# Four graph layers on one core: the tiled matmuls of a step in one run, O and h at its head, the transposed exponentials in its middle

## The reference

```
h  = relu(layernorm(x))                       # 128 x 384
q, k, v = h @ Wq + bq, h @ Wk + bk, h @ Wv + bv     # 6 heads of 64
p  = softmax(q @ k.T / 8, masked by adj)      # 6 x 128 x 128
x1 = x + (p @ v) @ Wf + bf
g  = relu(layernorm(x1))
hh = g @ W                                    # 12 heads of 32
a  = leaky_relu(tanh(hh)@w_src + (tanh(hh)@w_dst).T), no edge: -999
f  = elu(softmax(a) @ hh + b)                 # 12 x 128 x 128
gate = sigmoid(g @ H_w.T + H_b)
x2 = x1 + gate * f + (1 - gate) * g
```

## Time and profile before

| | |
|---|---|
| median of three runs | 2048.41 us |
| the profiled execution | 2048.47 us, of which the span is 2046.4 us |
| PE busy | 1979.5 us (97%) |
| ACT busy | 1953.5 us (95%) |
| DVE busy | 1813.4 us (89%) |
| POOL busy | 1629.2 us (80%) |
| mean granted TensorE clock | 0.988 of 2.4 GHz |
| ACT L525, first and last start | 84.0 and 2018.1 us |

### The profile page before, as it was taken

How to read it: one execution, slowest core, us unless ns; L and a number is a source line. 1 busy time by engine, 2 the same in 40 slices (tenths; PEclk the granted TensorE clock), 3 DMA queues, 4 the chain that set the end, 5 groups by cost and what they waited for, 6 DMA issues and landing times.

```text
span 2046.4 us, 58352 instructions
## 1 busy us (share of the span) xinstructions
PE 1979.5 (97%) x19596; PEld 1845.0 (90%) x19596; DVE 1813.4 (89%) x4117; ACT 1953.5 (95%) x6800; POOL 1629.2 (80%) x2859
## 2 busy tenths in 40 slices
PE   4999999999999999999999999999999999999983
PEld 4899999999999999999999999999999999999972
DVE  4689999999999999999999999999999999999884
ACT  3799999999999999999999999999999999999995
POOL 3478888888888888888888888878888878888864
PEclk9999999999999999999999999999999999999995
DMA  5012223323323222223432222222222222221122
GB/s 170 12 46 67 70 60 79 86 68 91 86 65 83 53 51 57 56 50 82 122 99 58 53 52 60 50 53 61 50 52 61 50 54 60 50 52 49 39 47 50
DMA packets 309330, 130.62 MB, mean 64 GB/s; under 512 B 229547, under 2 KB 308782, under 8 KB 309038
## 3 DMA queue, kind: packets, MB, share of 16 engines
q1 hardware_dynamic: 309038, 126.90, 24.8%
HBM read 69.42 MB, written 57.41 MB: 62 GB/s over the span
## 4 chain that ended last, share of the span: by engine, by line
ACT 49%; DVE 37%; PE 5%; issue 4%; POOL 2%; DMA 1%; DVEq 1%; SPq 1%; POOLq 0%
ACT LG L506 27%; ACT LA L500 14%; DVE LG L636 11%; DVE neg_max L640 10%; DVE LA L613 9%; DVE stats L617 3%; ACT cT_hi L558 2%; ACT QKT L514 2%; ACT v L566 2%; PE psum L731 2%; DVE rdenG L632 1%; DVE rden L611 1%; ACT sdT L572 1%; PE psum L741 1%; DMA xin<-x 1%
## 5 line engine op out<-in xcount | busy, mean ns | idle before, releaser
L506 ACT ACTIVATE LG<-LG,neg_max 128x128 f32<-128x128 f32 x1536 | 595.4, 392 | 15.9 <-DVE neg_max L640 8.8
L500 ACT ACTIVATE LA<-LA,neg_max 128x128 f32<-128x128 f32 x768 | 297.9, 400 | 0.0
L506 ACT ACTIVATION_READ_ACCUMULATOR LG<-LG,neg_max 128x1 f32 x1536 | 291.9, 190 | 0.0
L430 POOL TENSOR_TENSOR prod<-th,vec 128x384 f32<-128x384 f32 x256 | 254.3, 1017 | 6.9 <-ACT th L543 6.9
L636 DVE COPY_PREDICATED_SCALAR LG<-no_edge,no_edge_score 128x1536 f32 x128 | 245.5, 1918 | 7.4 <-ACT LG L525 7.3
L640 DVE TENSOR_REDUCE neg_max<-LG 128x12 f32<-128x1536 f32 x128 | 224.4, 1753 | 13.8
L741 PE MATMUL psum<-hT_hi,qk_hi 128*128 128x256 f32 x1152 | 212.4, 292 | 8.5 <-DVE hT_lo L655 8.5
L613 DVE TENSOR_TENSOR LA<-LA,rden 128x768 f32<-128x768 f32 x128 | 199.0, 1555 | 4.4
L741 PE MATMUL psum<-hT_hi,qk_lo 128*128 128x256 f32 x1152 | 200.8, 282 | 0.0
L741 PE MATMUL psum<-hT_lo,qk_hi 128*128 128x256 f32 x1152 | 200.6, 282 | 0.0
L525 ACT ACTIVATE LG<-psum 128x1536 f32<-128x1536 f32 x128 | 186.4, 1457 | 2.3 <-PE psum L814 2.3
(11 more groups left out here) (121 smaller groups left out, 6201.5 us busy)
## 6 DMA issues: line engine op xcount, KB each, us to landing
context<-gcT SPq DMA_DIRECT2D x512, 48.0 KB, 2.1
back<-context SPq DMA_DIRECT2D x128, 192.0 KB, 2.5
xin<-x SPq DMA_DIRECT2D x64, 192.0 KB, 2.4
x_mid<-x SPq DMA_DIRECT2D x64, 192.0 KB, 2.4
xin<-x_mid SPq DMA_DIRECT2D x64, 192.0 KB, 2.4
out<-x SPq DMA_DIRECT2D x64, 192.0 KB, 2.3
ahead<-stage SPq DMA_DIRECT2D x16, 288.0 KB, 3.5
stage<-w_qk SPq DMA_DIRECT2D x12, 192.0 KB, 3.6
```

The source lines that it names most:

```text
L430: last = pool.tensor_tensor(prod[:, i, :], th[:], vec[:, r.pair(k - 2), 2 + i, :], ALU.mult)
L500: last = act.activation(head, head, ACT.Exp, scale=-1.0, bias=neg_max[:, 0, h:h + 1], accum_out=rsum[:, h:h + 1])
L506: last = act.activation(head, head, ACT.Exp, bias=neg_max[:, 1, a:a + 1], accum_out=den[:, a:a + 1])
```

## The change

All engines' orders are written anew; the instructions of a full step are the same but for one. `v` is copied out of PSUM by VectorE (`tensor_copy`) and no more by ScalarE. The steps run from -2 to 136 and each stage has a new distance to k. TensorE's new order in a step is O(k-4), h(k-5), qk2(k), gpt1(k-7), sdT(k-6), pt(k-3), gpt2(k-7), gpt0(k-7), s(k-2), c(k-3), gc(k-7), z(k-6), gate(k-5), qk0(k), V(k-2), g_hT(k-4), m_hT(k+2), qk1(k). The banks are given out anew: s lies in 0 and 1, and the gate follows it in 0; c and pt lie in 4 and 5; z in 5, 6 and 7; O, gpt2, z and qk0 use bank 7 one after the other.

SyncE issues weight pieces 8 to 10 in step 0 and 11 to 13 in step 1, x of graphs 4 to 7 in steps 1 to 4, and the rest of the constants in step 2. The store of x2 now comes ahead of `context_back` in a step. GpSimd's part of the weight splitting (`split_ahead`) moves to the head of its step. For the last graph alone, Prelu, mask and maximum are done in three parts of four heads with semaphores of their own.

The diff, cut to its core (TensorE's, ScalarE's and VectorE's new orders are cut to the lines that the prediction speaks of):

```diff
-FIRST_STEP, STEPS_BEHIND = -7, 5
+FIRST_STEP, STEPS_BEHIND = -2, 9
...
-        SPLIT_STEPS = {-4: range(0, 3), -3: range(3, 6), -2: range(6, 8), -1: range(8, 11), 0: range(11, 14)}
+        LOAD_STEP = [0, 0, 0, 1, 1, 1]
+        SPLIT_STEPS = {-1: range(0, 3), 0: range(3, 6), 1: range(6, 8), 2: range(8, 11), 3: range(11, 14)}
...
-            for m in range(8, len(PIECES)):
-                load_piece(m)
-            for i in range(4, SLOTS):
-                load_x(x, i, i)
...
             def straight(k):
+                for m in range(8, len(PIECES)):
+                    if k == LOAD_STEP[m - 8]:
+                        load_piece(m)
+                for i in range(4, SLOTS):
+                    if k == max(i + -3, 0):
+                        load_x(x, i, i)
...
+                if r.has(k - 7):
+                    if k - 7 < ALL - 1:
+                        act.wait_ge(s["z_max"], r.done(k - 7))
+                    else:
+                        act.wait_ge(s["last_max2"], 1)
+                    graph_exps(range(8, 12)).then_inc(s["z_exp2"], 1)
...
-                if r.has(k + 1):
-                    act.wait_ge(s["m_v"], r.done(k + 1))
-                    act.activation(v[:, (k + 1) % 4, :], bank(1)[:, 0:D], ACT.Copy).then_inc(s["m_val"], 1)
...
+                        for q in range(QUADS):
+                            act.activation(LG[:, q * 4 * N:(q + 1) * 4 * N], bank(5 + q), ACT.Prelu, alpha=SLOPE).then_inc(s["z_leaky" if q == QUADS - 1 else f"last_leaky{q}"], 1)
...
+                if r.has(k - 3):
+                    dve.wait_ge(s["m_v"], r.done(k - 3))
+                    dve.tensor_copy(v[:, (k - 3) % 4, :], bank(6)[:, 0:D]).then_inc(s["m_val"], 1)
...
+                if r.has(k - 6):
+                    pe.wait_ge(s["g_sdR"], r.done(k - 6))
+                    wait_latest(pe, r, ("pt", k - 3), ("z_leaky", k - 7))
...
+                    for q in range(QUADS):
+                        rows = slice(q * GROUP, (q + 1) * GROUP)
+                        last = pe.matmul(bank(5 + q), sdT[rows, (k - 6) % 2, :], sdR[rows, (k - 6) % 2, :, :].rearrange("p a n -> p (a n)"), start=True, stop=True)
+                    last.then_inc(s["z_ps"], 1)
+                if r.has(k - 5):
+                    weights("gate", k - 5)
+                    pe.wait_ge(s["g_lo"], r.done(k - 5))
+                    wait_latest(pe, r, ("s_max", k - 2), ("gpt1", k - 7), ("m_lo", k + 1), ("g_gate", k - 6))
+                    pe.matmul(bank(0)[:, 0:D], ones[ROWS:128, :], hb3[ROWS:128, r.pair(k - 5), :], start=True, stop=False)
+                    nodes_times(bank(0)[:, 0:D], g_hi, g_lo, hg_hi, hg_lo, D, begun=True).then_inc(s["g_gate_ps"], 1)
                 if r.has(k):
+                    weights(f"c{(k - 2) % 2}0", k - (k - 2) % 2)
+                    wait_latest(pe, r, ("z_leaky", k - 6), ("gpt2", k - 7), ("x1", k - 4), ("qk0", k - 1))
+                    queries_keys(k - 2, 0, bank(7)).then_inc(s["qk_ps0"], 1)
```

More of the change, by code:

```diff
@@ L580, in setup @@
+                if r.has(k):
+                    act.wait_ge(s["qk_ps0"], r.done(k))
+                    queries_keys(r, k - 2, 0, bank(7)).then_inc(s["qk0"], 1)
+                if r.has(k - 8):
+                    act.wait_ge(s["y_min"], r.done(k - 8))
+                    act.activation(ey[:], ey[:], ACT.Exp).then_inc(s["y_exp"], 1)
             def setup(k):
@@ new lines, in step @@
+                if r.has(k - 3):
+                    dve.wait_ge(s["s_ps"], r.done(k - 3))
+                    dve.wait_ge(s["bias_mask"], r.done(k - 3))
+                    for i in range(MH):
+                        last = dve.tensor_tensor_reduce(LA[:, i * N:(i + 1) * N], bank(0 + i // KC)[:, (i % KC) * N:(i % KC + 1) * N],
+                                                        neg_bias[:, (k - 3) % 2, :], -1.0, HUGE, ALU.add, ALU.min, neg_max[:, 0, i:i + 1])
+                    last.then_inc(s["s_max"], 1)
@@ L749, in step @@
             def step(r, k):
[L750 to L753 removed]
+                if r.has(k - 4):
+                    weights("O", k - 4)
+                    pe.wait_ge(s["cT_lo"], r.done(k - 4))
+                    wait_latest(pe, r, ("qk0", k - 1), ("z_leaky", k - 7), ("gpt2", k - 8), ("x1", k - 5))
+                    nodes_times(bank(7)[:, 0:D], c_hi, c_lo, vf_hi, vf_lo, D).then_inc(s["o_ps"], 1)
@@ new lines, in step @@
+                if r.has(k - 2):
+                    if (k - 2) % 2 == 0:
+                        for i in range(3):
+                            pe.wait_ge(s[f"qk{i}"], r.done(k - 1))
+                    wait_latest(pe, r, ("gpt1", k - 7), ("m_lo", k + 1), ("g_gate", k - 6), ("s_max", k - 3))
+                    wait_latest(pe, r, ("qk1", k - 1), ("s_max", k - 3))
+                    for h in range(MH):
+                        i = place_of(h)
+                        rows = slice(64 * (h % 2), 64 * (h % 2) + 64)
+                        at = slice((k - 2) % 4 * N, ((k - 2) % 4 + 1) * N)
+                        last = pe.matmul(bank(0 + i // KC)[:, (i % KC) * N:(i % KC + 1) * N],
+                                         QKT[rows, h // 2, at], QKT[rows, KC + h // 2, at], start=True, stop=True)
+                    last.then_inc(s["s_ps"], 1)
@@ L866, in setup @@
+                if r.has(k):
+                    weights(f"c{(k - 2) % 2}1", k - (k - 2) % 2)
+                    wait_latest(pe, r, ("s_max", k - 2), ("qk1", k - 1))
+                    queries_keys(k - 2, 1, bank(1)).then_inc(s["qk_ps1"], 1)
             def setup(k):
-                for pair, at in ((0, -2), (1, 0)):
+                for pair, at in ((0, 1), (1, 3)):
                     if k == at:
```

617 lines of the change are left out of this document (298 added, 319 removed).

## The result

The changed kernel takes 2045.54 us in the median of 20 runs, the kernel before 2048.12 in 20 runs: ratio 0.9987, 95% interval 0.9981 to 0.9993. That is 2.6 us less, where 21 were forecast. In the profiled executions the span fell from 2046.4 to 2044.0 us.

The account below looks back on a forecast made before the run. TensorE's own instruction stream was taken to set the 15.28 us step, with a loop over ScalarE and VectorE as long; 2048.4 - 19.5 (steps) - 1.4 (end) + 0 (head) = 2027.5, said as 2027 us, range 2013 to 2050.

Parts of the forecast that it names:

- Part 1: TensorE's tiled run: four changes of tile shape a step instead of five, saving 0.20 us, step 15.08 us.
- Part 2: v copied by VectorE: ScalarE loses 0.38 us, needing at most 14.72 a step; VectorE gains 0.47, needing 14.84.
- Part 3: Old loop over ScalarE and VectorE: 14.3 us with the mask, 0.8 to spare, so it no longer matches TensorE's 15.28.
- Part 4: TensorE's next late waits, bias row (bank 0) and qk0 (bank 7): 0.04 us charged, step 15.12 us, 19.5 us saved.
- rival B: No change: new waits (0.2 us together) or VectorE growing to 15.25 take back the gain; 2047 us, chance 0.12.
- Rival C: Slower: the Prelu starts late and delays qk0 every step; at 0.4 us late 2071 us, chance 0.12.
- Part 6: Loads in order of need, the head: first qk matmul at 24 to 26.5 us, no gain, between -3 and +4.
- Part 7: Last softmax by thirds saves 0.6 us; the end in all -1.4 us, between +4 and -4.
- Part 5: VectorE and GpSimd at one time: scaling of LA left at 1.6 us, 0.6 less or 0.2 more.

Follow-up runs that it names:

- the first two experiments: Changed kernel with bank 0 signalled free after the third masked score: 2040.70 us; then also with the Prelu in two, bank 7 first: 2036.2 us.
- bank 7 sooner: Changed kernel with the gate's bias row waiting for three masked scores only, and the Prelu in two, bank 7 first: 2036.2 us.
- gT first: Changed kernel with the early semaphore for bank 0, and the g_hT transposes moved ahead of qk0 on TensorE: 2046.2 us.

## Why the prediction was wrong

By its own steps:

- **Part 1, the tiled run: right.** One shape change less; the waits show one for L766 instead of two. Its price of 0.20 is there in two pieces (medians of the steps from 500 to 1850 us): V's first two intervals fell from 0.449 to 0.354 us, and one last transpose fewer stands ahead of a change, with 0.109 us to what follows instead of 0.205. That is 0.095 + 0.096 = 0.19.
- **Part 2, v: right for the new order** (no change of time with v on ScalarE). By part 2's own count, the step less VectorE's waits, it came to 15.226 - 45.3 / 111 = 14.82 us, where 14.84 was forecast; the 14.41 of the window is its busy time, another count. For the old order it would have been wrong by 71 us.
- **Part 3, the old loop: right that it opens**, incomplete in what bound the kernel: GpSimd's loop over y had 0.05 us of air.
- **Part 4 is the step that failed.** Both waits were named with their place, and the sum charged 0.04 us for them together. The bias row cost 0.096 alone. I had it start 0.07 us behind z's first matmul and it starts 0.17 behind. The failing term is the handover itself: the masked scores are done 2.34 us after s starts (2.35 forecast) and z starts at 2.32 (2.31 forecast), but from the end of the scores to the bias row's matmul I took 0.03 us and it takes 0.147. The drain, which I put against it, gave back only 0.312 - 0.248 = 0.064 of 0.160. qk0's wait was hidden behind it and worth another 0.065, as the first two experiments show: with handovers in a row, the first to be late hides the next. A third, bank 2 behind hv, came up when the transposes were moved.
- **Part 4 also took the duration of every group as in the old order.** The pace of the 384-column groups changed with their place: h by 2.6 ns a matmul, V by 1.1, gate by 0.8, in all (2.6 + 1.1 + 0.8) x 9 = 0.041 us a step. With it 15.281 - 0.20 + 0.096 + 0.041 = 15.218, and 15.226 was measured. The forecast of 15.12 was short by these two terms. This was rival B in its size, 2047 us. Of its mechanism half is there: waits took back 0.096 us, one of the three that it named, and the slower pace, which it did not name, 0.041. That it came close is in part luck. Rival C was wrong: the Prelu had 0.39 us of air.
- **Part 6, the head, was wrong by 2.4 us.** The first qk matmul started at 24.86 us, inside the forecast 24 to 26.5, but I followed the head only to there. The first graph then takes 90.02 - 24.86 = 65.2 us to its first maximum instead of 61.9. In these windows TensorE is busy for 62.0 us after and 56.9 before: with z late in the step, 5.1 us more of its work, for later graphs, lies ahead; that this is the cause was not tested. And I had named the wait for hb_row as the new head of the chain without pricing its removal, 9.3 us.
- **Part 7, the end: wrong by 2 us.** Thirds 0.24 instead of 0.6; z behind gc some 0.6 to 1.2 us, which had been weighed in words only.
- The splitting at the head of GpSimd's step was not priced. The 112 full steps from the seventh maximum to the 119th take 2.6 us more than 112 medians, 1.8 before, nearly all in the steps that split.

Part 5 had the duration about right (1.47 us in the median for 1.6) but read it as a slowing. The trace shows a wait for the rest of the other engine's instruction. In the changed kernel, ey on GpSimd, the scaling of LA on VectorE, and hM:

```profile
1009.70 1.02 POOL L427 TENSOR_TENSOR ey<-ey,hG 128x384 f32<-128x384 f32 x1
...
1010.08 1.46 DVE L689 TENSOR_TENSOR LA<-LA,rden 128x768 f32<-128x768 f32 x1
...
1010.72 1.35 POOL L432 TENSOR_SCALAR hM<-xin,rstd,shift 128x384 f32<-128x384 f32 x1
```

The scaling starts while ey runs and ends 0.81 to 0.82 us after ey's end in the 117 steps where they meet, however long ey still had to go (mostly 0.64 to 0.79). Alone it takes 0.957. hM, behind it, lasts 1.35 us instead of 0.66 and ends 0.54 after the scaling. The Trainium skill (SBUF — State Buffer, SBUF: two separate sides) says that such a pair lock one another out for a whole instruction. The trace agrees. What the lock costs depends on when the second one starts: here 0.5 us, since half of ey and more is still to run. Beside it VectorE still had 45.3 / 111 = 0.41 us a step of waiting for s, so nothing shows that the lock set the step.

## What to carry to other kernels

When a resource's own stream is the bound and a new order gives banks or buffers to new users, price every handover on it in a row, each with the one before it already eased; one late by 0.1 us hides the next. Charge each with the time from the reader's end to the matmul that waits for it, here 0.15 us. Ask of each first use behind the handover whether a part of the reader's work would free it: here two finer semaphores, with one instruction split, gave 9.3 us where the new order alone gave 2.6. And follow a new head past the first matmul to the first result, with every wait for a small DMA that the new first step puts ahead of it.

## What the runs showed of the hardware

- From the last matmul of one tile shape to the first of the next TensorE takes 0.20 us: gc (32 columns) to z (32 rows) 0.205, to a full-array transpose 0.203, and that single transpose to z 0.26. With no change it is 0.109 between transposes, so about 0.10 is the change's, and a first group of 384 columns behind it takes 0.10 more (0.449 us over two intervals instead of 0.354). The Trainium skill (TensorEngine Tiling (Array Packing), Key Properties) says that a switch of mode drains the array; these runs put the price to it, and agree in that c to gc, one mode, is 0.09 us.
- The same 128x384 float32 matmul follows the last after 173.4 ns or after 176 to 177, at a granted clock of 1.00. Mostly it goes by what was ahead: behind a change of shape, or behind such a group, 173.4; behind groups of 256 columns, and on through the next groups of 384, 176 to 177. Why is open, and there are exceptions: in the changed kernel V, behind qk0, ran at 173.2 in most steps and at 176 to 177 in the others, with a stall of 0.16 us two groups ahead; with bank 7 sooner, without a stall, it was 177.2 in every step.
- The first 256-column group behind full-array transposes takes 0.320 us over its first two intervals where others of its kind take 0.240, but it starts 0.028 us behind the last transpose instead of 0.109. The two cancel.
- A weight load that waits for VectorE to be done with a bank starts 0.116 us after VectorE's last instruction on it ends (the bias row behind the masked scores, changed kernel), and 0.115 in the kernel with gT first (the transposes behind hv).
